# VectorE in place of GpSimd for the multiply by the reciprocal sums in the last attention layer

## What is computed

```
x      = layernorm(builder, g1, beta1);  base_n = layernorm(base_state, g1, beta1)
q, k, v = heads(x, Wq), heads(base_n, Wk), heads(base_n, Wv)        # 8 heads of 32
scores = einsum('bhqd,bhkd->bhqk', q, k) / sqrt(32)
attn   = softmax(scores)                                            # exp, row sum, divide
x      = residual + einsum('bhqk,bhkd->bhqd', attn, v) @ W_o.T + b_o
U      = (layernorm(x, g2, beta2) @ W_in.T + b_in) @ Bmat
s_t    = silu(s_{t-1} @ A.T) + u_t          for t in 0..127
out    = x + states @ Cmat + mean(program_probs) @ W_prog.T + b_prog
```

## Time and profile before

| what | us |
|---|---|
| median of 3 runs | 878.3 |
| lowest and highest run | 874.64, 880.05 |
| the profiled execution, time | 875.15 |
| its span | 873.4 |
| mean granted clock of TensorE, share of full speed | 0.971 |

### The profile page before, as it was taken

How to read it: one execution, slowest core, us unless ns; L and a number is a source line. 1 busy time by engine, 2 the same in 40 slices (tenths; PEclk the granted TensorE clock), 3 DMA queues, 4 the chain that set the end, 5 groups by cost and what they waited for, 6 DMA issues and landing times.

```text
span 873.4 us, 17026 instructions
## 1 busy us (share of the span) xinstructions
PE 776.8 (89%) x5876; PEld 618.9 (71%) x5876; DVE 545.7 (62%) x2252; ACT 429.2 (49%) x1760; POOL 336.4 (39%) x344
## 2 busy tenths in 40 slices
PE   0799898799889987998899989998989987999997
PEld 0588676588778876887688778876778766875564
DVE  1457667757865886587748785876477748341023
ACT  0636264554745664566455655668236536242332
POOL 4123444342634453445344634465234625220000
PEclk9789998899999999999999999998999998999999
DMA  8600100000000000000000000000000000001012
GB/s 326 233 8 7 37 1 20 14 14 1 14 8 24 3 13 8 1 26 14 7 2 25 13 2 1 26 1 2 1 1 1 2 0 2 1 1 25 1 44 55
DMA packets 16633, 21.42 MB, mean 25 GB/s; under 512 B 3869, under 2 KB 13090, under 8 KB 15906
## 3 DMA queue, kind: packets, MB, share of 16 engines
q1 hardware_dynamic: 16258, 20.06, 7.1%
q10 hardware_dynamic: 288, 0.26, 0.2%
HBM read 17.69 MB, written 2.10 MB: 23 GB/s over the span
## 4 chain that ended last, share of the span: by engine, by line
PE 70%; DVE 18%; issue 4%; POOL 2%; DMA 2%; ACT 2%; SPq 1%; DVEq 0%; POOLq 0%
PE work_bank L599 21%; PE work_bank L590 20%; PE work_bank L734 6%; DVE probs L967 4%; DVE probsT L1069 4%; PE work_bank L582 3%; PE scores_bank L819 3%; PE work_bank L650 3%; PE scores_bank L628 3%; PE scores_bank L560 3%; PE work_bank L806 2%; DVE xn L985 2%; DVE stats L1004 1%; DMA bias<-in_mask 1%; POOL probs L850 1%
## 5 line engine op out<-in xcount | busy, mean ns | idle before, releaser
L850 POOL TENSOR_TENSOR probs<-probs,rtotal 128x512 f32<-128x512 f32 x160 | 164.6, 1041 | 221.3 <-DVE rtotal L1059 221.0
L1164 ACT ACTIVATE probs<-probs,nmx 128x128 f32<-128x128 f32 x512 | 197.9, 391 | 80.7 <-DVE nmx L967 80.3
L1069 DVE COPY probsT<-work_bank 128x512 f32<-128x512 f32 x160 | 106.4, 679 | 18.1 <-PE work_bank L734 17.4
L599 PE MATMUL work_bank<-L_w,hidden 128*128 128x256 f32 x512 | 113.9, 380 | 0.0
L734 PE MATMUL work_bank<-ident,probs 128*128 128x128 f32 x640 | 97.7, 292 | 16.4 <-POOL probs L850 10.2
L599 PEld LDWEIGHTS work_bank<-L_w,hidden 128*128 128x128 f32 x512 | 96.0, 190 | 14.1 <-ACT hidden L1219 1.7
L850 POOL TENSOR_TENSOR rstd<-veps,half 128x2 f32<-128x2 f32 x64 | 45.4, 711 | 154.5 <-DVE veps L1012 154.0
L734 PEld LDWEIGHTS work_bank<-ident,probs 128*128 128x128 f32 x640 | 76.6, 149 | 36.7 <-POOL probs L850 17.5
L1164 ACT ACTIVATION_READ_ACCUMULATOR probs<-probs,nmx 128x1 f32 x512 | 97.4, 190 | 0.0
L582 PE MATMUL work_bank<-ident,xn 128*128 128x128 f32 x256 | 42.5, 290 | 28.5 <-DVE xn L985 28.4
L967 DVE CUSTOM_DVE_ANT_0 probs<-scores_bank,causal 128x128 f32<-128x128 f32 x256 | 57.2, 285 | 8.9 <-PE scores_bank L628 8.8
(11 more groups left out here) (167 smaller groups left out, 1463.0 us busy)
## 6 DMA issues: line engine op xcount, KB each, us to landing
L_w<-in_L_w SPq DMA_DIRECT2D x4, 1024.0 KB, 11.1
x_in<-in_x SPq DMA_DIRECT2D x8, 256.0 KB, 2.8
c_in<-in_ctx SPq DMA_DIRECT2D x8, 256.0 KB, 2.8
cT<-in_ctxT SPq DMA_DIRECT2D x8, 256.0 KB, 3.1
rows<-in_rows SPq DMA_DIRECT2D x1, 1280.0 KB, 7.5
bias<-in_mask SPq DMA_DIRECT2D x8, 128.0 KB, 2.3
out<-x_all SPq DMA_DIRECT2D x8, 128.0 KB, 2.4
L_wq<-in_L_wq SPq DMA_DIRECT2D x3, 256.0 KB, 9.3
```

The lines of the kernel that those rows point to most:

```text
L599: mm = nc.tensor.matmul(d[:, b * D:b * D + D], xT, w, start=(n == 0), stop=(n == len(todo) - 1))
L850: return nc.gpsimd.tensor_tensor(out, a0, a1, op)
L1069: nc.vector.tensor_copy(turn_slot(s, i, key), d[:].rearrange("p (j k) -> p j k", j=4))\
L1164: ins = nc.scalar.activation(e_at[slot][:, j, :], src, ACT.Exp, bias=nmx[:, slot, j:j + 1], scale=1.0 if s == "C" else -1.0, accum_out=tot ...
```

## The change

The set SCALED names the stages whose quads are multiplied on VectorE, and it holds C alone. There the item rec issues the reciprocal, waits for it through link, and then multiplies the 128x512 probabilities in place; rsummed is counted up by the multiply. The turns of C wait for rsummed in place of weighed. The 32 items C*.nrm.* are taken out of GPSIMD_ORDER; the order of all other items on all engines is as before, and A, B and M keep their multiplies on GpSimd.

```diff
@@ GPSIMD_ORDER @@
-M5.rstd.cr M5.crg M5.skip G6.rstd.c C3.rstd.x7 C3.x7b M5.nrm.s A6.rstd.x2 A6.x2b C4.rstd.x6 C4.x6b A7.nrm.0 A7.nrm.2
-A7.nrm.1 A7.nrm.3 B5.nrm.0 B5.nrm.2 B5.nrm.1 B5.nrm.3 B5.nrm.4 B5.nrm.5 B5.nrm.6 A7.xb M6.rstd.x3 B5.nrm.7 M6.x3b
-A7.nrm.4 A7.nrm.5 M6.nrm.a A7.nrm.6 A7.nrm.7 C4.nrm.0 B5.rstd.x5 C4.nrm.1 B5.x5b C4.nrm.2 C4.nrm.3 M6.rstd.cr M6.crg
...
+M5.x3b A6.nrm.4 A6.nrm.5 M5.nrm.a H7.rstd.x A6.nrm.6 A6.nrm.7 B4.rstd.x5 B4.x5b M5.rstd.cr M5.crg M5.skip G6.rstd.c
+C3.rstd.x7 C3.x7b M5.nrm.s A6.rstd.x2 A6.x2b C4.rstd.x6 C4.x6b A7.nrm.0 A7.nrm.2 A7.nrm.1 A7.nrm.3 B5.nrm.0 B5.nrm.2
+B5.nrm.1 B5.nrm.3 B5.nrm.4 B5.nrm.5 B5.nrm.6 A7.xb M6.rstd.x3 B5.nrm.7 M6.x3b A7.nrm.4 A7.nrm.5 M6.nrm.a A7.nrm.6
+A7.nrm.7 B5.rstd.x5 B5.x5b M6.rstd.cr M6.crg M6.skip G7.rstd.c C4.rstd.x7 C4.x7b M6.nrm.s A7.rstd.x2 C5.rstd.x6 A7.x2b
...
+SCALED = "C"
...
                 elif kind == "turn":
-                    ready(weighed, WEIGHED[s, i, ("nrm", key)])
+                    if s in SCALED:
+                        ready(rsummed, RSUMMED[s, i, ("rec", key)])
+                    else:
+                        ready(weighed, WEIGHED[s, i, ("nrm", key)])
...
                         ins = nc.vector.reciprocal(m_rtotal[:], m_total[:])
+                    elif s in SCALED:
+                        n = quad_slot(s, i, key)
+                        links += 1
+                        link(nc.vector.reciprocal(rtotal[:, n, :], total[:, n, :]), links)
+                        ins = nc.vector.tensor_tensor(e_at[n], e_at[n], rtotal[:, n, :].unsqueeze(2).broadcast_to([P, 4, P]),
+                                                      ALU.mult)
                     else:
```

More of the change, by code:

```diff
@@ L198 @@
 A3.nrm.1 A3.nrm.2 C0.rstd.x6 A3.nrm.3 C0.x6b B1.nrm.0 B1.nrm.1 B1.nrm.2 B1.nrm.3 B1.nrm.4 B1.nrm.5 B1.nrm.6 A3.xb
[L199 to L207, removed]
@@ L208 @@
-A6.nrm.4 A6.nrm.5 M5.nrm.a H7.rstd.x A6.nrm.6 A6.nrm.7 B4.rstd.x5 B4.x5b C3.nrm.0 C3.nrm.1 C3.nrm.2 C3.nrm.3
-M5.rstd.cr M5.crg M5.skip G6.rstd.c C3.rstd.x7 C3.x7b M5.nrm.s A6.rstd.x2 A6.x2b C4.rstd.x6 C4.x6b A7.nrm.0 A7.nrm.2
-A7.nrm.1 A7.nrm.3 B5.nrm.0 B5.nrm.2 B5.nrm.1 B5.nrm.3 B5.nrm.4 B5.nrm.5 B5.nrm.6 A7.xb M6.rstd.x3 B5.nrm.7 M6.x3b
-A7.nrm.4 A7.nrm.5 M6.nrm.a A7.nrm.6 A7.nrm.7 C4.nrm.0 B5.rstd.x5 C4.nrm.1 B5.x5b C4.nrm.2 C4.nrm.3 M6.rstd.cr M6.crg
-M6.skip G7.rstd.c C4.rstd.x7 C4.x7b M6.nrm.s A7.rstd.x2 C5.rstd.x6 A7.x2b C5.x6b B6.nrm.0 B6.nrm.1 B6.nrm.2 B6.nrm.3
@@ L213 @@
[L213 to L216, removed]
+M2.rstd.x3 B1.nrm.7 M2.x3b A3.nrm.4 A3.nrm.5 M2.nrm.a H4.rstd.x A3.nrm.6 A3.nrm.7 B1.rstd.x5 B1.x5b M2.rstd.cr M2.crg
@@ new lines @@
+M2.skip G3.rstd.c C0.rstd.x7 C0.x7b M2.nrm.s A3.rstd.x2 A3.x2b C1.rstd.x6 C1.x6b A4.nrm.0 A4.nrm.2 A4.nrm.1 A4.nrm.3
+B2.nrm.0 B2.nrm.2 B2.nrm.1 B2.nrm.3 B2.nrm.4 B2.nrm.5 B2.nrm.6 A4.xb M3.rstd.x3 B2.nrm.7 M3.x3b A4.nrm.4 A4.nrm.5
+M3.nrm.a H5.rstd.x A4.nrm.6 A4.nrm.7 B2.rstd.x5 B2.x5b M3.rstd.cr M3.crg M3.skip G4.rstd.c C1.rstd.x7 C1.x7b M3.nrm.s
+A4.rstd.x2 A4.x2b C2.rstd.x6 C2.x6b A5.nrm.0 A5.nrm.2 A5.nrm.1 A5.nrm.3 B3.nrm.0 B3.nrm.2 B3.nrm.1 B3.nrm.3 B3.nrm.4
+B3.nrm.5 B3.nrm.6 A5.xb M4.rstd.x3 B3.nrm.7 M4.x3b A5.nrm.4 A5.nrm.5 M4.nrm.a H6.rstd.x A5.nrm.6 A5.nrm.7 B3.rstd.x5
@@ new lines @@
+B3.x5b M4.rstd.cr M4.crg M4.skip G5.rstd.c C2.rstd.x7 C2.x7b M4.nrm.s A5.rstd.x2 A5.x2b C3.rstd.x6 C3.x6b A6.nrm.0
+A6.nrm.2 A6.nrm.1 A6.nrm.3 B4.nrm.0 B4.nrm.2 B4.nrm.1 B4.nrm.3 B4.nrm.4 B4.nrm.5 B4.nrm.6 A6.xb M5.rstd.x3 B4.nrm.7
+M5.x3b A6.nrm.4 A6.nrm.5 M5.nrm.a H7.rstd.x A6.nrm.6 A6.nrm.7 B4.rstd.x5 B4.x5b M5.rstd.cr M5.crg M5.skip G6.rstd.c
+C3.rstd.x7 C3.x7b M5.nrm.s A6.rstd.x2 A6.x2b C4.rstd.x6 C4.x6b A7.nrm.0 A7.nrm.2 A7.nrm.1 A7.nrm.3 B5.nrm.0 B5.nrm.2
+B5.nrm.1 B5.nrm.3 B5.nrm.4 B5.nrm.5 B5.nrm.6 A7.xb M6.rstd.x3 B5.nrm.7 M6.x3b A7.nrm.4 A7.nrm.5 M6.nrm.a A7.nrm.6
@@ L217 @@
+A7.nrm.7 B5.rstd.x5 B5.x5b M6.rstd.cr M6.crg M6.skip G7.rstd.c C4.rstd.x7 C4.x7b M6.nrm.s A7.rstd.x2 C5.rstd.x6 A7.x2b
+C5.x6b B6.nrm.0 B6.nrm.1 B6.nrm.2 B6.nrm.3 B6.nrm.4 B6.nrm.6 B6.nrm.5 B6.nrm.7 M7.rstd.x3 M7.x3b M7.nrm.a B6.rstd.x5
+B6.x5b M7.rstd.cr M7.crg M7.skip C5.rstd.x7 C5.x7b M7.nrm.s C6.rstd.x6 C6.x6b B7.nrm.0 B7.nrm.1 B7.nrm.2 B7.nrm.3
+B7.nrm.4 B7.nrm.5 B7.nrm.6 B7.nrm.7 B7.rstd.x5 B7.x5b C6.rstd.x7 C6.x7b C7.rstd.x6 C7.x6b C7.rstd.x7 C7.x7b
 """
```

## The result

The changed kernel takes 883.8 us (median of 9 runs, 882.7 to 887.5), the kernel before 877.6 (9 runs beside them). The ratio is 1.0077, with a 95% interval of 1.0057 to 1.0098: slower, by less than 1%. The profiled execution has a span of 881.0 us where that of before had 873.4.

The account below looks back on a forecast made before the run. TensorE's hand-written order plus its holes bounds the time. C0 to C3 0, C4 +1.5, C5 +1.5, C6 +2.3, C7 -0.3, clock +1.6 give +6.6 on 878.3: 884.9 us, range 877.5 to 892.

Parts of the forecast that it names:

- The price: VectorE's multiply takes 0.69 us; all queued behind is 0.76 us later per quad, the turn 0.36 us earlier if nothing else holds it.
- C0 to C3, 0: First four pairs, 16 quads: the multiplies fit VectorE's idle time before each reciprocal, cost 0.
- C4, +1.5: Pair C4: two multiplies ahead of max.2 delay exp.2, the gelu and TensorE's ffn1.2, 2 x 0.76 = 1.5 us.
- C5's queue, +1.5: Pair C5: multiplies ahead of flip.o and x5's xn cost 0.25 + 3 x 0.76, less 1.07 from an unstretched xn: 1.5 us.
- C5's clock, +1.6: TensorE at C5: idle from about 682.5 to 684.6, one more fall of the granted clock, 3.63 - 1.99 = 1.6 us.
- C6, +2.3: Pair C6: multiplies precede max.2 and max.3, and B7.mix.1's eviction comes behind all four; what follows is 2.3 us late.
- more falls of the clock: Rival: TensorE's busy share in C6 gets thinner, one or two more falls, 886.5 to 888.1 us; chance 0.10.
- C7, -0.3: Pair C7: on the chain from exp.3 through multiply and turn, mix comes at about 779.1 in place of 779.37, -0.3 us.
- A dear multiply: Rival: VectorE's multiply takes 1.01 us, 4.2 us on top, 889.1; only some stretched beside GpSimd, 886.3; chance 0.10 for dear or blocked.

Follow-up runs that it names:

- the second (1.0098 of 875.7): The unaltered changed kernel run once more against the kernel before, for a second profile: 1.0098, 885.1 us.
- The filled kernel: The changed kernel plus matmuls that nobody reads in TensorE's holes of C5 and C6: 1.0064 of the kernel before, 882.2 us.
- the extra multiplies: Kernel before plus one unread VectorE multiply behind each reciprocal of C4, C5 and C6: 1.0110, 885.2 us; of C0 to C3 instead: 0.9995, 874.8 us.
- the reordered kernel: The changed kernel with three moves in VectorE's order, at C4, C5 and C6: 1.0074 of the kernel before, 882.5 us.
- 2.14 alone: Kernel before with only C6's four multiplies on VectorE: 1.0021, 876.8 us; its stretch at C6 is 2.14 us longer.

## Why the prediction was right, and where it was not

The forecast was 884.9 us and the measured median is 883.8. Its difference, +6.6 us, stands against +6.1 in the first comparison and +8.6 in the second (1.0098 of 875.7). Step by step:

- **The price.** 0.69 was taken for the multiply, 0.70 measured. In C6 reciprocal and multiply pass at a pace of 0.81 us (737.12, 737.93, 738.74), where 0.84 was worked out. The hop from the reciprocal's start to the turn is 0.94 to 0.95 (737.12 to 738.06, 737.93 to 738.88), where 0.93 was expected.
- **C0 to C3, 0.** Right: 0.9975 and 0.9995, and no turn late.
- **C4, +1.5.** Right as a sum. What was to show it was not: the hole before ffn1.2 was to grow from 1.88 to 3.4 us and grew to 2.32, since two earlier waits of TensorE took the other 1.1 us (1.16 to 1.67, 0.24 to 0.80). The stretch is 1.53 against 0 and -0.15 against -1.65, at equal clock 1.5 both times. The sign of the clock there is not the change's: in some executions of any of these kernels the fall at ffn1.2 is missing, and 1.65 us with it.
- **C5's queue, +1.5.** Nearly right. The first matmul of the flip is 2.1 us later relative to what came before it (-1.85 to +0.26 between the two traces), the third 1.54 (-0.31 against -1.85): xn's give-back arrives with its second half. The filled kernel gives 1.3.
- **C5's clock, +1.6.** The fall was foreseen and its size was wrong; this is the term that was mis-sized. I priced it as the slow ffn1.2 of before's C4, 3.63 - 1.99. That fall happened to begin at ffn1.2 and to end after about 4 us. The one in C5 began in the hole ahead of the flip and lasted for about 10 us (681.5 to 692, read from short stretches of the granted clock), over the flip, the turns, the score, ffn1.2 and what follows: 5.7 - 1.5 = 4.2 us. All five executions with a longer hole in C5 have it (four with the multiplies there, one with the extra multiplies), at 5.6 to 5.8 us in all (in the reordered kernel with 2.4 us of queue and about 7 us of low clock), and it is gone in the one trace where the hole is filled.
- **C6, +2.3.** Right as a queue term: 2.14 alone. In the whole change C6 is 4.43 and 3.77, since the clock falls there too (739.8 to 749.5 in the first, some 3.5 us of it in the second). The sum had nothing for that; it was the rival *more falls of the clock*, and it came. But kernels that leave C6 alone also lose 1.25 to 1.51 there in four of eight executions, so only a part of it belongs to the change.
- **C7, -0.3.** Right in sign and size where it can be seen, -0.36 and -0.37, but in the whole change, in both executions, it is lost again at the norm that follows: xn of x7 starts 1.27 us behind GpSimd's rstd instead of 0.92. Why isn't known.
- **A dear multiply.** It exists, but rarely: 1.01 us at 604.13, where GpSimd's tensor_tensor (603.34 to 604.60) runs beside it, 0.69 to 0.70 for the other 31, also for the two that meet an rstd of GpSimd and were thought to be able to stretch. In C4 it is hidden behind ffn1.2. It is rare because this change takes GpSimd's multiplies away; the extra multiplies, which meet them, are stretched more often. This agrees with the Trainium skill (SBUF — State Buffer, Who interferes with whom), by which VectorE with two SBUF inputs contends with GpSimd; and VectorE: DVE Perf Modes, whose (N+151)/0.96 ns gives 0.69, agrees with the undisturbed ones.

So why did the time come out right with one term 2.6 us too small? From 590 us on the changed kernel's two executions are 9.9 and 10.2 us longer than the first of before (the rows of the table added up), the timings say 6.1 and 8.6, and I said 6.6 on a base of 878.3 where later medians of before were 875.3 to 875.8. What the traces show beyond the timings, 1.6 to 3.8 us, is as large as one or two falls of the clock that come and go, and as the differences before 590 us. One profile of each kernel doesn't fix such a mean. That part isn't settled: the closeness of 884.9 to 883.8 is partly that a term too small met a base too high, while the ratio's estimate, 1.0075, is inside both intervals on its own.

## What to carry to other kernels

An instruction moved to another engine is priced by that engine's queue at the place where it lands, not by its mean load: VectorE at 62% took 16 multiplies for nothing in one stretch, and 12 in another, 8.4 us of work, made the kernel 6 to 9 us slower. Before such a move, list for each place the idle time just ahead of the new instruction, and what is queued behind it. And price a new hole on the engine that sets the time by what the clock may do over the following 10 us, not over the one group of instructions behind the hole.

## What the runs showed of the hardware

- Between 550 and 760 us, the length of a stretch of low granted clock (0.50) differs from place to place: about 3.5, 7 or 10 us. One of about 3.5 us cost 1.2 to 1.65 us, one of 7 us in C5 3.24, those of about 10 us some 4.2 in C5 and 2.3 in C6.
- Whether it falls isn't settled by the program alone. The same stretch, with the same instructions, shows the fall in some executions and not in others (-1.20 and -1.65 in the table), and then the rest of the trace agrees to 0.05 us. In C5 the fall came in 5 of 5 executions with a hole of 1.7 to 2.6 us, in 1 of 8 with before's hole of 1.0, and not in the one execution in which fillers ran in the hole.
- VectorE's and GpSimd's tensor_tensor of 128x512 stretch each other when they overlap: VectorE's from 0.69 to 1.01 us in the changed kernel and from 0.66 to as much as 1.41 for the extra multiply, GpSimd's from 1.04 to as much as 1.49 beside the extra multiply.
- A VectorE tensor_scalar, not only a tensor_tensor, is stretched beside GpSimd: xn takes 0.73 us alone, 1.46 and 1.80 beside GpSimd's multiplies. The same section of the Trainium skill (SBUF — State Buffer, Who interferes with whom) names tensor_scalar among the operations that can take the shared port in a two-port mode; the rows agree with that, without showing the mode.
